# A mixture-of-experts kernel: the weighted sum of experts moves from VectorE to ScalarE and GpSimd

## What is computed

```python
x = x + ssm(layernorm(x))        # selective state space: 64 inner channels, 8 states
x = x + ffn(layernorm(x))
x = x + attention(layernorm(x))  # 16 heads of 8, chunks of 10, 25 rows to the left
x = x + ffn(layernorm(x))

def ffn(x):                      # 8 experts, all of them for every row, F = 512
    g, u = einsum("bsh,ehf->ebsf", x, w_gate), einsum("bsh,ehf->ebsf", x, w_up)
    expert_out = einsum("ebsf,efh->ebsh", silu(g) * u, w_down)
    cw = softmax(x @ w_router) * softmax(x @ w_gating / 0.1)
    cw = cw / (sum(cw) + 1e-09)
    return einsum("ebsh,bse->bsh", expert_out, cw)
```

## Time and profile before

| | |
|---|---|
| median of three runs | 1425.51 us (1422.82 to 1425.74) |
| profiled execution, its own time | 1425.63 us |
| its span in the trace | 1423.8 us |
| mean granted clock of TensorE | 0.992 |
| TensorE busy | 1364.1 us (96%), weight loads 1179.9 us |
| VectorE busy | 951.1 us (67%) |
| ScalarE busy | 773.1 us (54%) |
| GpSimd busy | 517.1 us (36%) |

### The profile page before, as it was taken

How to read it: one execution, slowest core, us unless ns; L and a number is a source line. 1 busy time by engine, 2 the same in 40 slices (tenths; PEclk the granted TensorE clock), 3 DMA queues, 4 the chain that set the end, 5 groups by cost and what they waited for, 6 DMA issues and landing times.

```text
span 1423.8 us, 31460 instructions
## 1 busy us (share of the span) xinstructions
PE 1364.1 (96%) x12700; PEld 1179.9 (83%) x12700; DVE 951.1 (67%) x2294; ACT 773.1 (54%) x1049; POOL 517.1 (36%) x517
## 2 busy tenths in 40 slices
PE   4889999999999999999999989999999999999998
PEld 3788777888888888887888878888888888888887
DVE  6766777775876668568675676757856675576543
ACT  6565648653565556637475665556634563365321
POOL 4260564533423453247312751236503421341000
PEclk9999999999999999999999999999999999999999
DMA  6210231003010310131003300050003000300000
GB/s 233 59 31 17 67 79 32 20 12 78 2 47 16 71 24 1 47 68 35 9 2 83 64 2 9 1 116 32 2 1 73 8 2 1 71 9 2 9 1 8
DMA packets 70235, 51.39 MB, mean 36 GB/s; under 512 B 4140, under 2 KB 60508, under 8 KB 70092
## 3 DMA queue, kind: packets, MB, share of 16 engines
q1 hardware_dynamic: 70060, 49.38, 14.4%
q10 hardware_dynamic: 32, 0.02, 0.0%
HBM read 44.92 MB, written 4.46 MB: 35 GB/s over the span
## 4 chain that ended last, share of the span: by engine, by line
PE 79%; DVE 8%; POOL 5%; issue 4%; ACT 3%; DMA 0%; DVEq 0%; POOLq 0%
PE pd L1125 26%; PE pg L289 8%; PE pu L289 7%; PE pg L291 7%; PE pg L290 7%; PE pu L290 7%; PE pu L291 7%; PE att_ps L766 2%; POOL arena L713 2%; PE att_ps L791 2%; DVE h L1234 1%; POOL arena L715 1%; PE pd L1117 1%; DVE x L1222 1%; PE side_ps L326 1%
## 5 line engine op out<-in xcount | busy, mean ns | idle before, releaser
L1185 ACT ACTIVATE h<-pg 128x512 f32<-128x512 f32 x512 | 304.3, 598 | 601.8 <-PE pg L291 599.6
L1125 PEld LDWEIGHTS pd<-w_down,h 128*128 128x128 f32 x3840 | 483.4, 192 | 33.9 <-issue 4.1
L1125 PE MATMUL pd<-w_down,h 128*128 128x128 f32 x3840 | 489.7, 276 | 1.3 <-DVE x L1222 1.1
L1234 DVE TENSOR_TENSOR h<-h,pu 128x512 f32<-128x512 f32 x512 | 344.8, 678 | 214.9 <-PE pu L291 204.8
L289 PE MATMUL pg<-ffn_x_hi,w_gate_hi 128*128 128x512 f32 (+1 forms) x544 | 248.3, 456 | 1.1 <-DVE ffn_x_lo L376 1.1
L289 PE MATMUL pu<-ffn_x_hi,w_up_hi 128*128 128x512 f32 (+1 forms) x544 | 210.3, 387 | 12.6 <-DVE h L1234 12.5
L290 PE MATMUL pu<-ffn_x_lo,w_up_hi 128*128 128x512 f32 (+1 forms) x544 | 208.4, 383 | 0.0
L291 PE MATMUL pg<-ffn_x_hi,w_gate_lo 128*128 128x512 f32 (+1 forms) x544 | 208.3, 383 | 0.0
L290 PE MATMUL pg<-ffn_x_lo,w_gate_hi 128*128 128x512 f32 (+1 forms) x544 | 208.2, 383 | 0.0
L291 PE MATMUL pu<-ffn_x_hi,w_up_lo 128*128 128x512 f32 (+1 forms) x544 | 207.9, 382 | 0.0
L976 POOL TENSOR_TENSOR att_arena<-att_arena,r_sums 128x512 f32<-128x512 f32 (+1 forms) x72 | 72.6, 1008 | 272.9 <-DVE r_sums L856 272.8
(11 more groups left out here) (222 smaller groups left out, 1440.1 us busy)
## 6 DMA issues: line engine op xcount, KB each, us to landing
arena<-bc_spread SPq DMA_DIRECT2D x56, 256.0 KB, 4.6
att_arena<-v_rows SPq DMA_DIRECT2D x64, 144.0 KB, 3.9
att_arena<-v_rows SPq DMA_DIRECT2D x64, 128.0 KB, 3.7
arena<-in_x SPq DMA_DIRECT2D x8, 256.0 KB, 3.1
x<-in_x SPq DMA_DIRECT2D x8, 256.0 KB, 3.5
w_down<-in_w_down SPq DMA_DIRECT2D x8, 256.0 KB, 5.0
v_rows<-att_arena SPq DMA_DIRECT2D x8, 256.0 KB, 2.3
out<-x SPq DMA_DIRECT2D x8, 256.0 KB, 2.2
```

The costliest lines, as they stand in the source:

```text
L1125: last = nc.tensor.matmul(pd[:, t * P:(t + 1) * P], h_b[:, d % NH, t * P:(t + 1) * P], wd[:, d % NCH, :], start=d % CPE == 0 and t == 0, s ...
L1185: nc.scalar.activation(h_b[:, c % NH, :], pg[c % 2][:, :], ACT.Silu).then_inc(gate_done, 1)
L1234: nc.vector.tensor_tensor(h, h, pu[d % 2][:, :], ALU.mult).then_inc(h_done, 1)
```

## The change

In mains 1 to 15 (experts 8 to 127 in the count over all mains) VectorE no longer takes the down bank out. ScalarE does it (`weigh`), with four activations of the kind Copy, each of 128x128 with the weight's column as its scale, from `pd` into one of two tiles `x_add`, which are parts of `k_room` that held weights only while the kernel starts. They stand ahead of the silu of slot 4e + 8 and count up a new semaphore, `weighed`; TensorE's next down products wait for that. GpSimd then adds the tile to x with one instruction of 128x512 (`add`, at the same slot ahead of what is due there), and this counts up `summed` by four. ScalarE waits for `summed` of two experts before, as there are two tiles. The routing waits for `weighed` before it overwrites a `mix` that ScalarE reads. 480 instructions of VectorE become 480 of ScalarE and 120 of GpSimd; main 0 stays as it was.

```diff
--- before.py
+++ after.py
@@ -183,6 +183,8 @@
 
         axf = q_room[:, 1, :]
 
+        x_add = [k_room[:, 2 + i, 0:L].rearrange("p (t d) -> p t d", t=TT) for i in range(2)]
+
         dec_0 = [pt_flat[:, 0, :], pt_flat[:, 1, :]] + [xb[i][:, :, :].rearrange("p t d -> p (t d)") for i in (2, 3)]
         room = [att_ar[:, N_S + i * L:N_S + (i + 1) * L] for i in range(8)]
         xb_0, zb_0, dx_0 = room[0:3]
@@ -209,7 +211,7 @@
         b_used, dx_done, dec_first, scan_first = sem("b_used"), sem("dx_done"), sem("dec_first"), sem("scan_first")
         y_first, mid_out, mid_moved = sem("y_first"), sem("mid_out"), sem("mid_moved")
         g_full, u_full, gate_done, h_done = sem("g_full"), sem("u_full"), sem("gate_done"), sem("h_done")
-        down_done, summed = sem("down_done"), sem("summed")
+        down_done, weighed, summed = sem("down_done"), sem("weighed"), sem("summed")
         att_full, att_free = ([sem(f"att_{v}{i}") for i in range(2)] for v in ("full", "free"))
         side_full, side_free = [sem("side_full")], [sem("side_free")]
         ln_sems = {k: (sem(f"{k}_stats"), sem(f"{k}_rstd"), sem(f"{k}_rows")) for k in ("ssm_ln", "att_ln", "ffn_ln")}
@@ -384,6 +386,8 @@
                                                ALU.subtract), name)
                 yield t0 + 7
                 dve.wait_ge(route_exp, 2 * (n + 1))
+                if m > 2:
+                    dve.wait_ge(weighed, TT * E * (m - 2))
 
                 link.count(nc.vector.reduce_sum(sums[:, :, 0:2], lgs, AX))
                 link(nc.vector.tensor_tensor(cw, lgs[:, :, 0, :], lgs[:, :, 1, :], ALU.mult))
@@ -1107,7 +1111,10 @@
                         if d == 0:
                             pe.wait_ge(wd_loaded, 16 * E)
                         if d % CPE == 0 and d:
-                            pe.wait_ge(summed, TT * (d // CPE))
+                            if d <= NCH:
+                                pe.wait_ge(summed, TT * (d // CPE))
+                            else:
+                                pe.wait_ge(weighed, TT * (d // CPE - E))
                         if d < NCH:
 
                             for j in range(2):
@@ -1169,7 +1176,22 @@
                     act.wait_ge(w_loaded[j], 16)
                     nc.scalar.copy(w_part(j, 0), w_raw[j]).then_inc(w_hi, 1)
 
+                def weigh(e):
+
+                    m = e // E
+                    if e % E == 0:
+                        act.wait_ge(mix_ready, HEAD_OF[m, 0] + 1)
+                    act.wait_ge(down_done, CPE * (e + 1))
+                    if e >= E + 2:
+                        act.wait_ge(summed, TT * (e - 1))
+                    for t in range(TT):
+                        nc.scalar.activation(x_add[e % 2][:, t, :], pd[:, t * P:(t + 1) * P], ACT.Copy,
+                                             scale=mix[m % 2][:, t, e % E:e % E + 1]).then_inc(weighed, 1)
+
                 def chunk(c):
+                    d = c - 1 - LAG
+                    if d >= NCH and d % CPE == CPE - 1:
+                        weigh(d // CPE)
                     if c < 0:
                         if 0 <= c + SETUP - 7 < 2 * E:
                             split_w(c + SETUP - 7)
@@ -1200,28 +1222,17 @@
 
                 def weigh(e):
 
-                    m = e // E
-                    x = xb[ORDER[m][0] % NXB]
-                    if m and e % E == 0:
-                        dve.wait_ge(mix_ready, HEAD_OF[m, 0] + 1)
-                    elif e in (0, E // 2):
+                    x = xb[ORDER[0][0] % NXB]
+                    if e in (0, E // 2):
                         dve.wait_ge(mix_ready, 2 * e // E + 1)
                     dve.wait_ge(down_done, CPE * (e + 1))
-                    if m == 0:
-
-                        for q in range(TT):
-                            i, t = 2 * (e % (E // 2)) + q // 2, 2 * e // E * (TT // 2) + q % 2
-                            if e or q >= 2:
-                                dve.wait_ge(summed, TT * e + q - 1)
-                            nc.vector.scalar_tensor_tensor(x[:, t, :], pd[:, q * P:(q + 1) * P], mix[0][:, t, i:i + 1],
-                                                           x[:, t, :], ALU.mult, ALU.add).then_inc(summed, 1)
-                        return
-                    for t in range(TT):
-                        if e:
-                            dve.wait_ge(summed, TT * (e - 1) + t + 1)
-                        nc.vector.scalar_tensor_tensor(x[:, t, :], pd[:, t * P:(t + 1) * P],
-                                                       mix[m % 2][:, t, e % E:e % E + 1], x[:, t, :],
-                                                       ALU.mult, ALU.add).then_inc(summed, 1)
+
+                    for q in range(TT):
+                        i, t = 2 * (e % (E // 2)) + q // 2, 2 * e // E * (TT // 2) + q % 2
+                        if e or q >= 2:
+                            dve.wait_ge(summed, TT * e + q - 1)
+                        nc.vector.scalar_tensor_tensor(x[:, t, :], pd[:, q * P:(q + 1) * P], mix[0][:, t, i:i + 1],
+                                                       x[:, t, :], ALU.mult, ALU.add).then_inc(summed, 1)
 
                 def chunk(c):
                     if c < 0:
@@ -1233,7 +1244,7 @@
                         dve.wait_ge(u_full, d + 1)
                         nc.vector.tensor_tensor(h, h, pu[d % 2][:, :], ALU.mult).then_inc(h_done, 1)
                     d = c - 1 - LAG
-                    if d >= 0 and d % CPE == CPE - 1:
+                    if 0 <= d < NCH and d % CPE == CPE - 1:
                         weigh(d // CPE)
                     yield
 
@@ -1281,7 +1292,16 @@
                     nc.gpsimd.tensor_tensor(w_part(j, 1), w_raw[j], w_part(j, 0).bitcast(F32),
                                             ALU.subtract).then_inc(w_lo, 1)
 
+                def add(e):
+                    x = xb[ORDER[e // E][0] % NXB]
+                    pool.wait_ge(weighed, TT * (e - E + 1))
+                    pool.wait_ge(summed, TT * e)
+                    nc.gpsimd.tensor_tensor(x[:, :, :], x[:, :, :], x_add[e % 2], ALU.add).then_inc(summed, TT)
+
                 def chunk(c):
+                    d = c - 1 - LAG
+                    if d >= NCH and d % CPE == CPE - 1:
+                        add(d // CPE)
                     if c < 0 and 0 <= c + SETUP - 8 < E:
                         split_w(c + SETUP - 8)
```

## The result

The changed kernel takes 1454.61 us (median of 4 runs, 1452.79 to 1457.99) against 1425.45 in the same comparison: a ratio of 1.0211, with a 95% interval of 1.0189 to 1.0234. It is slower by 29 us, in the direction of the forecast but five times as much, and far outside its range.

A forecast was written before the change was run, and what follows sets the result against it. TensorE was taken as the bound, with 21.1 us idle between 148 and 1010 us, where its waits decide. Delays less 2.9 of gains gave +5.46 us: 1431.1 us forecast, chance 0.44, range 1421.5 to 1439.5.

The forecast's parts named there:

- Prices and the end: Four ScalarE copies 1.23 us, GpSimd's add 1.28; after the last expert, before the store, they cost +1.46 us without cover.
- Steady state: In quiet pieces the copies cost nothing; 1010 to 1414 us, where TensorE idled only 0.2 us, would stay full.
- The upper end of the range: 1439.5 us: the general stand, plus 1.4 for copies at 1.56 where four of the terms hang on them.
- The gains, -2.9: VectorE's freed time before late h multiplies: 302.52 gives 0.5, 634.15 0.7, 998.69 0.6, 833.20 1.1; 374.90 and 647.48 nothing.
- The first step of sequence 2, +1.0: At 154.21 us the add behind L715 makes VectorE's L662 stand 1.0 us, on TensorE's 2.0 us wait for h.
- The later steps and the norm, +2.3 and +1.3: Adds delay GpSimd's later state steps up to 190 us, +2.3, and the next expert layer's norm rows, 198 to 207, +1.3.
- The places at 605 and 803 us, +1.0 and +1.3: At 605.58 the add holds L662, +1.0; at 802.8 it comes between L969 and L976 and delays L865, +1.3.
- the sum: All terms: 1.46 + 1.0 + 2.3 + 1.3 + 1.0 + 1.3 - 2.9 = +5.46 us.
- The hold: A GpSimd add reading SBUF makes VectorE's L662 beside it stand 1.0 us; priced at 154.21 and 605.58 us.
- the rival in which it is general: All nine steps with the add behind L715 cost TensorE 1.0 us, 7 more: 1438.1 us, chance 0.05.
- The clock: As many drops of the granted clock as before; one drop would cost some 3.4 us.

The follow-up runs named there:

- the run without adds: The changed kernel with GpSimd's adds left out, so that who waited for them waits for ScalarE's copies: 1423.74 us, ratio 0.9987.
- the ladder: Medians from copies without adds, 1423.7 us, through adds cut to 8 columns, 1427.9, and 1.285 us memsets for adds, 1443.4, to the full change, 1454.6.
- the longer memset: The changed kernel with a GpSimd memset of 1420 columns, 1.285 us, in place of each add; same place and waits, reads nothing: 1443.43 us.
- run of the nine adds: The kernel before, plus one SBUF-reading GpSimd add into scratch directly behind L715 in nine state steps, waiting for nobody: 1434.38 us; with memsets instead, 1426.75.

## Why the prediction was wrong, by its own steps

**Prices and the end: right.** Four copies take 1.14 us (1.23 forecast), the add 1.297 (1.28). The end, ScalarE and GpSimd, changed kernel:

```profile
1446.94 1.14 ACT L1188 ACTIVATE k_room<-pd,mix 128x128 f32<-128x128 f32 x4 [3.99 <-PE pd L1132]
1448.21 1.26 POOL L1299 TENSOR_TENSOR x<-x,k_room 128x512 f32<-128x512 f32 x1 [3.86 <-ACT k_room L1188]
```

From 1446.94 to 1449.47 are 2.53 us, against 1.13 before: 1.40 more, 1.46 forecast. Steady state: the copies cost nothing there, as forecast, but the stretch did not stay full. From 1200 to 1440 us TensorE has 2.0 us of new waits, 1.6 of them for a norm's rows that wait for GpSimd's root. (The upper end of the range comes out at 1439.4 by its own terms, as 4 x 0.33 is 1.3 and not 1.4; nothing hangs on it.)

**The gains, -2.9: near in size by luck, wrong in place.** The copies alone gained 1.7 in all. TensorE's waits fell by 1.0 us behind 302.52, where half had been forecast, and by 1.0 behind 374.90, where nothing had; behind 634.15 and 998.69 nothing came. With the adds in, 0.4 us of it is left, at 833.20.

**The first step of sequence 2, +1.0: right.** L666 stood 1.06 us longer than 0.69, and TensorE's wait there went from 2.0 to 3.0.

**The later steps and the norm, +2.3 and +1.3: right.** L717 of the third step came at 174.74 instead of 168.89, 5.85 later. But 3.00 of this are the first stretch's, by which everything here is late, and about 1.0 the first step's; that leaves 1.8, and I had 1.9. The wait of the last step came as a late h, 2.84 us at 191.33, in place of the 1.5 for L673, so 1.3 more and not 2.3; the norm's went from 1.2 to 2.77, 1.6 more. The third stretch is still longer by 8.0 us: it has further waits (249.42, below) and 4.6 us of the lower clock.

**The places at 605 and 803 us, +1.0 and +1.3: right.** TensorE waits 0.97 us longer at the first, and 0.94 us at the second, where it had not waited.

**The step that failed is the count of places.** I priced an add only at six places where GpSimd's row already came last in the trace of before, and at the end, and put the length of the other hundred at nothing without a reason. TensorE's waits of 0.3 us and more (the brackets of its timeline, added up from 140 us on) are 22.0 us before, 22.0 in the run without adds and 41.0 in the changed kernel. Of the 19.0 new ones 5.8 stand at the places of the sum, which had 6.9 for them. The other 13.2 stand where the sum had nothing or a gain: at the state steps of the later sequences, beside the attention, and at a norm of the last stretch. One of them in the kernel before:

```profile
957.95 0.50 PE L289 MATMUL pu<-ffn_x_hi,w_up_hi 128*128 128x512 f32 x1 [1.29 <-DVE h L1234]
```

And in the changed kernel, where the second row is the same place:

```profile
249.42 0.70 PE L291 MATMUL pu<-ffn_x_hi,w_up_hi 128*128 128x512 f32 x1 [1.91 <-DVE h L1245]
...
981.38 0.50 PE L291 MATMUL pu<-ffn_x_hi,w_up_hi 128*128 128x512 f32 x1 [2.27 <-DVE h L1245]
```

At the place of the first row the kernel before has no wait of 0.3 us, and the run without adds one of 0.61. GpSimd's share of the span, 36% before, says how much it works and not how soon its results are wanted. The waits behind this, in the kernel before, without adds, and in the changed one:

```profile
DVE arena L662 <- POOL arena L715: 36.1, 17, 3.4
...
DVE ffn_rows L312 <- POOL rstd_ffn_ln L320: 5.1, 6, 1.2
...
PE pu L289 <- DVE h L1234: 12.5, 11, 2.0
```

```profile
DVE arena L666 <- POOL arena L719: 48.3, 19, 3.8
...
DVE ffn_rows L314 <- POOL rstd_ffn_ln L322: 4.9, 6, 1.2
...
PE pu L291 <- DVE h L1246: 12.2, 12, 2.0
```

```profile
DVE arena L666 <- POOL arena L719: 55.5, 20, 5.7
...
DVE ffn_rows L314 <- POOL rstd_ffn_ln L322: 17.9, 11, 4.2
...
PE pu L291 <- DVE h L1245: 26.8, 19, 3.0
```

The run without adds has to stand between, since VectorE, relieved of the multiply-adds, comes earlier and so waits longer by itself. Of the 19.4 us by which it waits longer for the state steps' products 12.2 are of that kind, and TensorE loses nothing by them (its waits for h are 12.5 and 12.2). With the adds come 7.2 more there, 13.0 for the norms' roots and 14.6 of TensorE's waits for h. In the order of the ladder the larger part of GpSimd's price is the length, 15.6 us, for which the sum had 2.3, two times 1.3 and the end.

**The hold: the right mechanism at too few places.** I gave it 1.0 at two steps, and the rival in which it is general 0.05. It is nearly general: at eight of the nine steps L666 took 1.16 to 1.77 us. Against the longer memset, with the same waits, TensorE waits longer behind at least five of these (3.03 against 2.00 us behind the first), and L666 and L667 take 73.1 us against 59.7; the ladder gives reading 11.2 us of the program. The argument against the rival, that the add has run by the time VectorE comes, fails for two reasons. At five steps VectorE waits for L719 and starts the moment that it ends, which is also when the add starts. At three the add itself was late, since it waited for the copies, and met a late VectorE. One of these, in the changed kernel, and the same step with an add that waits for nobody (run of the nine adds, L667 is L662):

```profile
844.76 1.29 POOL L1299 TENSOR_TENSOR x<-x,k_room 128x512 f32<-128x512 f32 x1 [1.70 <-issue]
...
844.96 1.65 DVE L666 SCALAR_TENSOR_TENSOR arena<-arena 128x512 f32<-128x512 f32 x1
```

```profile
826.06 1.26 POOL L724 TENSOR_TENSOR scratch<-w_down 128x512 f32<-128x512 f32 x1
...
829.16 0.68 DVE L667 SCALAR_TENSOR_TENSOR arena<-arena 128x512 f32<-128x512 f32 x1
```

In the second the argument holds. The rival's own 1438.1 was too low as well, since it took over the lengths and the clock of the forecast.

**The clock: a term that I set to zero.** "As many drops as before" became 8.8 us of busy time in the profile. 2.8 of them lie in the first stretch, which the change doesn't touch. In the third, TensorE's new waits and the lower clock stand together:

```profile
214.00:224.00 10.00, 7.24 (x123) 6.13 (x122) 5.68 (x14) 7.48 (x13) 1.04 (x1) 0.83 0.01 2
244.00:254.00 10.00, 8.09 (x67) 6.11 (x66) 5.08 (x11) 9.88 (x15) 3.28 (x4) 0.83 0.43 107
```

These windows of 10 us hold 2.8 and 1.9 us of idle time of TensorE and a mean clock of 0.83 each, so a part of them at the lower of its two levels, against a mean of 1.00 in this stretch before. The nine adds show the same as an experiment: 2.1 us more idle, 4.6 us more busy.

## What to carry to other kernels

An engine's busy share doesn't say that it has room: before work is moved to it, look up who waits for its results, and count one instruction's length for each of its places in that row, not only where it comes last already. To see what the new work itself delays, compare with a kernel that leaves it out: an engine that was relieved comes earlier and waits longer without any loss. A GpSimd instruction that reads SBUF, put directly behind the one that releases VectorE, started together with what it released and held it. Moving it behind GpSimd's next instruction gained nothing here; moving it to where GpSimd need not wait for its input gained 15 us, and cutting it there 7 more. And where TensorE is the bound, the wait alone is the lower bound of its price: new waits of 1.9 and 2.8 us stood here beside a mean clock of 0.83.

## What was not expected of the hardware

- The hold isn't one of two-input instructions alone. A norm's rows (L314, four pieces that each read one SBUF tensor and two columns) took 3.46 us with GpSimd's L722 and L1299 beside them (above), and 1.11 where GpSimd rests. The scan was held as well, from 1349 to 1486 ns on the mean. The forecast had named both beside its rival, without a price. L314 at a quiet place of the changed kernel:

```profile
1352.46 1.11 DVE L314 TENSOR_SCALAR ffn_rows<-x,mv_ffn_ln,rstd_ffn_ln 128x128 f32<-128x128 f32 x4 [0.90 <-POOL rstd_ffn_ln L322]
```

- It goes both ways: with the add in four pieces VectorE gets in, and then the 1.70 us of GpSimd's pieces become 3.07.
- A memset of 1420 columns, 1.285 us, holds nothing that the groups show: L668 at 828 ns, and L669 (the scan) at 1302.
- 484 us of waiting in GpSimd's row cost 4.1 us where what then ran was 0.267 us long. With the full add, taking 251 of 448 us of waiting away gave 15.
